# Mixed inputs of values and gate: products on ScalarE, sums on POOL, and ScalarE's order within a block

## The reference, cut to what matters

```python
xx = shift(x) - x                       # the token before minus this one
xk = x + xx * time_maa_k; xv = x + xx * time_maa_v
xr = x + xx * time_maa_r; xg = x + xx * time_maa_g
r, k, v = heads(xr @ Wr.T), heads(xk @ Wk.T), heads(xv @ Wv.T)
g = gelu(xg @ Wg.T)
# in chunks of 64 tokens, for each of 16 heads:
y  = (r @ k) * Wmat @ v + r @ state * wb
state = ws * state + (k * wk) @ v
out = (groupnorm(y) * ln_w + ln_b) * g @ Wo.T
```

## Time and profile before

| what | us |
|---|---|
| median of 3 runs (lowest, highest) | 846.95 (845.86, 848.41) |
| the profiled execution | 846.3 |
| its span, first to last instruction | 844.6 |
| busy TensorE, weight loads | 814.7, 674.5 |
| busy VectorE, ScalarE, POOL | 505.7, 464.4, 468.3 |

### The profile page before, as it was taken

One profiled execution on the slowest core, in us unless ns is written; L12 is line 12 of the kernel. 1 busy time (PEld: TensorE's weight loads), 2 busy tenths in 40 slices (PEclk: granted clock), 3 DMA queues, 4 the chain that ended last, 5 costly groups with the idle time before them and its releaser, 6 DMA issues. The chain is left out here.

```text
span 844.6 us, 17509 instructions
## 1 busy us (share of the span) xinstructions
PE 814.7 (96%) x6291; PEld 674.5 (80%) x6291; DVE 505.7 (60%) x1286; ACT 464.4 (55%) x860; POOL 468.3 (55%) x529
## 2 busy tenths in 40 slices
PE   5999999999999989899999999999999999999997
PEld 4777787777777667678998788898788899788886
DVE  6789988899998886343543543544443545353441
ACT  4478877778787667264543543644552544453331
POOL 6445577777777857475444356453436452535215
PEclk9999999999999999999999999999999999999999
DMA  5852032213111121546333334342415442413114
GB/s 163 334 209 70 28 108 68 76 52 96 40 40 48 58 91 72 178 157 135 101 70 40 110 95 70 95 113 27 124 60 79 121 106 26 95 35 44 20 14 50
DMA packets 50746, 74.30 MB, mean 88 GB/s; under 512 B 5072, under 2 KB 42448, under 8 KB 50640
## 3 DMA queue, kind: packets, MB, share of 16 engines
q1 hardware_dynamic: 35760, 53.72, 19.2%
q0 software_dynamic: 14592, 19.18, 13.6%
q10 hardware_dynamic: 288, 0.01, 0.0%
HBM read 38.67 MB, written 34.22 MB: 86 GB/s over the span
## 5 line engine op out<-in xcount | busy, mean ns | idle before, releaser
L1648 POOL DMA_INDIRECT out<-ysb,index x80 | 124.7, 1558 | 145.6 <-DVE ysb L1887 111.1
L2001 PE MATMUL p<-xh,whi 128*128 128x512 f32 (+2 forms) x504 | 185.4, 368 | 1.4 <-POOL wlo L1637 0.5
L1863 DVE TENSOR_TENSOR hid<-gated,p 128x512 f32<-128x512 f32 (+1 forms) x126 | 81.0, 643 | 176.2 <-ACT gated L1710 176.2
L2003 PE MATMUL p<-xh,wlo 128*128 128x512 f32 (+2 forms) x504 | 185.3, 368 | 0.0
L2002 PE MATMUL p<-xl,whi 128*128 128x512 f32 (+2 forms) x504 | 184.6, 366 | 0.0
L2027 PE MATMUL py<-w,hh 128*128 128x512 f32 x448 | 162.5, 403 | 4.2 <-DVE hl L1132 3.7
L1710 ACT ACTIVATE gated<-p 128x512 f32<-128x512 f32 (+1 forms) x126 | 70.8, 562 | 157.4 <-PE p L2003 152.8
L1637 POOL TENSOR_TENSOR wlo<-wraw,whi 128x448 fp32r<-128x448 f32 x56 | 70.8, 1267 | 89.8 <-ACT whi L1696 84.4
L2001 PEld LDWEIGHTS p<-xh,whi 128*128 128x128 f32 x504 | 94.7, 188 | 19.2 <-issue 3.5
L2026 PE MATMUL py<-w,hl 128*128 128x256 f32 x384 | 108.5, 283 | 0.0
L2002 PEld LDWEIGHTS p<-xl,whi 128*128 128x128 f32 x504 | 94.8, 188 | 15.2
(11 more groups left out here) (215 smaller groups left out, 1430.7 us busy)
## 6 DMA issues: line engine op xcount, KB each, us to landing
wraw<-in_w SPq DMA_DIRECT2D x24, 896.0 KB
disp<-wraw SPq DMA_DIRECT2D x16, 662.5 KB, 8.2
xtok<-disp SPq DMA_DIRECT2D x16, 530.0 KB, 4.8
x_ring<-in_x SPq DMA_DIRECT2D x16, 256.0 KB, 3.3
out<-x SPq DMA_DIRECT2D x16, 256.0 KB
xtok<-disp SPq DMA_DIRECT2D x8, 265.0 KB
out<-ysb,index POOLq DMA_INDIRECT x80
disp<-row,slot_i POOLq DMA_INDIRECT x64
```

Of the source, the lines that this page charges most:

```text
L1648: nc.gpsimd.indirect_dma_start(out, bass.IndirectOffsetOnAxis(ap=index[e.const % 2][:, t:t + 1], axis=0), ysb[j % NY][:], None, compute_op ...
L1863: nc.vector.tensor_tensor(hid[k][:, 0:w], gated[k][:, 0:w], p3[k][:, 0:w], ALU.mult).then_inc(hid_ready, 1)
L2001: nc.tensor.matmul(dst[:, 0:w], hi[m][:, wcut], xh[xcut], start=(kt == 0), stop=False)
L2003: ins = nc.tensor.matmul(dst[:, 0:w], lo[m][:, wcut], xh[xcut], start=False, stop=(kt == KT - 1))
```

## The change

For each block, the mixed inputs 2 and 3 are now made in two steps. ScalarE computes the products of both (`mixed_part`: two ACTIVATE Copy instructions with a scale for each, four in all), and POOL adds xT to each (`mixed_add`: one addition of 128 x 512 for each). VectorE's two fused instructions for values leave its loop, and POOL's two products for the gate leave POOL's. `shifted`, which overwrites diff, now waits for both additions.

Three steps of ScalarE move in its loop: `weight_high` from behind `square_y` to ahead of `turned1`; `normed2` from behind `scaled` to behind `column`; `normed1` from behind `gate` to the end. The four products stand where `normed1` stood. On POOL the scatter of tile 0 moves ahead of `gated`.

```diff
+        def mixed_add(b, k):
+            if 0 <= b < STEPS:
+                pool.wait_ge(part_ready[k], b + 1)
+                nc.gpsimd.tensor_tensor(mixed[k][:], mixed[k][:], xT[b % 2][:, :, 1:], ALU.add).then_inc(mixed_ready[k], 1)
...
             norm2(c - 2)
-            mixed_g(c + 1)
-            gated(c - 1)
             if c < TAIL - 1:
                 scatter(c - 4, range(0, 1))
+            mixed_add(c + 1, 2)
+            gated(c - 1)
+            mixed_add(c + 1, 3)
             decayed_r(c + 1)
...
+        def mixed_part(b, k):
+            if 0 <= b < STEPS:
+                act.wait_ge(diff_ready, b + 1)
+                wait(act, proj_done[k], b)
+                if b == 0:
+                    act.wait_ge(maa_in, 16)
+                for c in range(KT):
+                    ins = nc.scalar.activation(mixed[k][:, c, :], diff[:, c, :], ACT.Copy, scale=maa_sb[:, k, c:c + 1])
+                ins.then_inc(part_ready[k], 1)
...
+            weight_high(c - 4)
             turned1(c + 1)
             group_rstd(c - 1)
             logit_exp(c - 2)
             gate(c)
-            normed1(c + 2)
+            mixed_part(c + 1, 2)
+            mixed_part(c + 1, 3)
             scaled(c - 1)
-            normed2(c - 2)
             receptance(c + 1)
...
             square_y(c)
-            weight_high(c - 4)
             keep_y(c)
             column(c + 1)
+            normed2(c - 2)
             keep_logits(c + 1)
+            normed1(c + 2)
...
-                wait(dve, mixed_ready[3], b)
+                for k in (2, 3):
+                    wait(dve, mixed_ready[k], b)
...
-            mixing(c + 1, 2)
```

More of the change, by code:

```diff
@@ L408, in phase_a @@
     diff_ready = sem("diff_ready")
+    part_ready = {k: sem(f"part_ready{k}") for k in (2, 3)}
     mixed_ready = [sem(f"mixed_ready{k}") for k in range(4)]
@@ L577, in decayed_r @@
                     rdecay[:].unsqueeze(2).to_broadcast([P, KT, TPS, Q]), ALU.mult).then_inc(rdec_ready, 1)
-        def mixed_g(b):
+        def mixed_add(b, k):
             if 0 <= b < STEPS:
[L581 to L588, removed]
+                pool.wait_ge(part_ready[k], b + 1)
+                nc.gpsimd.tensor_tensor(mixed[k][:], mixed[k][:], xT[b % 2][:, :, 1:], ALU.add).then_inc(mixed_ready[k], 1)
         def weight_low(i):
```

## The result

The changed kernel takes 852.62 us (median of 7 runs, 850.73 to 854.85), the kernel before beside it 845.86 (7 runs). The ratio is 1.0073, with a 95% interval of 1.0057 to 1.0089. The forecast of 843.5 was wrong, and so was its range: the time lies 5.2 us above the end of it, and 3.2 above the one rival that was slower than before. The profiled execution took 850.73, with a span of 848.5 where the kernel before has 844.6.

A forecast was written before the change was run, and what follows sets the result against it. TensorE's own list was taken to bound the attention at 18.03 us a block, with the expert stage untouched. Terms 1.9 + 1.2 + 0.5 - 0.1 = 3.5 us off 846.3 gave 842.8, median 843.5; range 841.3 to 847.4.

The forecast's parts named there:

- What bounds the kernel: Attention blocks: TensorE's own list sets 18.03 us a block; nine blocks can give back about 4.1 us.
- state_a and the masks: Loop blocks: state_a runs ahead of POOL's addition, 0.4 us instead of 1.24; TensorE's wait for masks goes: 1.9 us off.
- The residual's lag: Ahead of group sums: r_dec starts earlier and stops holding back the residual addition: 1.2 us off, bounds 0 and 1.2.
- ScalarE and z: Loop blocks: ScalarE can hold four more products; zg is ready 0.3 us before TensorE wants it.
- I count all of this at 0: Loop blocks: the other moved steps of ScalarE and POOL cost nothing, except 0.1 us lost for zg.
- The first: Rival, group sums: the residual's lag is not POOL's and stays; 1.2 us of the sum goes: 844.7; chance 0.17.
- The second: Rival, loop: state_a meets the new addition, r_dec still holds the residual; 0.4 us is left: 846.5; chance 0.20.
- The third: Rival: z behind four products makes project_o wait 0.45 us in each of 13 blocks: 849.4; chance 0.08.
- The fourth: Rival: waits for k_dec shrink as well, and the last block gives 1.1 us: 842.0; chance 0.10.
- Start, end and expert stage: Block from 279.81 gives 0.5 us, bounds -0.5 and 1.1; start-up, written-out end and expert stage keep their times.

The follow-up runs named there:

- The kernel that has all of it: Changed kernel with all four scatters ahead of POOL's first addition, and k_dec ahead of logit_max and stats2 on VectorE: 838.21 us, 0.9915 of before.
- 841.27: Changed kernel with POOL's weight piece moved ahead of the scatter of tile 1: 841.27 us, 0.9944 of before.
- 839.49: Changed kernel with all four scatters of a block moved ahead of POOL's first addition: 839.49 us, 0.9931 of before.
- a run that left POOL alone: Kernel before the change, with k_dec moved ahead of logit_max and stats2 on VectorE: 845.07 us, 0.9984 of before.
- the run with one input: Changed kernel with L1118 taking the counts in PSUM instead of slotf in SBUF, leaving the capacity rule out of the slots: 848.36 us, 1.0025 of before.

## Why the prediction was wrong, step by step

**What bounds the kernel.** Right: a block of 18.03, about 4.1 us to be had in nine blocks, and no more. The kernel that has all of it shows it.

**state_a and the masks.** Right in mechanism and size. The pair takes 0.41 and starts at T+5.6, ahead of the first addition by 1.0 us; the masks no longer wait. The prediction had a POOL addition hold a VectorE instruction with two inputs in SBUF, and this held wherever the runs put the two together. The pair of state_b (L1029) now meets zg (L617): the pair ends at 199.10 and zg at 199.05, and it takes 1.42 instead of 0.40, which the prediction didn't mention; it falls ahead of the residual's wait of 1.79 and costs nothing.

**The residual's lag.** The size is right, -1.3 against -1.2, and the reason isn't shown. The prediction had r_dec hold the residual, because the residual began 0.37 to 0.44 us after it. With k_dec earlier in the kernel before, r_dec begins as near or nearer, and there is no lag. With the piece ahead of the DMAs the residual begins 0.56 to 0.60 us into the weight piece in eight blocks, and is on time and takes 0.42. The lag went in every run of another kernel but for 0.1 us where the values are back on VectorE, whose pair ends late there. So this term came out by luck, as far as the runs tell: what made the residual late in the kernel before stays open.

**ScalarE and z.** Right. zg is ready at T+9.67, and TensorE takes it at T+10.36: the cover is 0.7 where the prediction had 0.3, because four products take 1.69 and the next starts after 1.60, not 1.98:

```profile
194.97 1.69 ACT L685 ACTIVATE mixed<-diff,maa_sb 128x256 f32<-128x256 f32 x4
196.57 1.08 ACT L821 ACTIVATE z<-yn,lnb_sb,lnw_sb 128x256 f32<-128x256 f32 x2
```

**The step that failed** is "I count all of this at 0", of what the change moves on POOL. The prediction had looked for who waits for each moved step, and found nobody early enough. It had not looked for what each POOL instruction now runs beside. It had both facts for it: that POOL holds small VectorE instructions until its end, and that the weight piece does so to L1075. It applied them to state_a and the residual, and never walked down VectorE's list for instructions that weren't late yet. What the runs showed in place of the 0: the product L1118, or one of the three ahead of it, is held for 1.6 to 1.8 us in each of eight blocks, k_dec is late behind it, and scores wait 11.2 us more.

That walk would have been close, too. By the prediction's own times r_dec starts at T+11.3, so that the second DMA of tile 1 starts at about T+14.1, and the product, 1.33 us behind the residual at T+12.4, at T+13.7: free, by 0.3 us. In the run r_dec starts at T+10.68. The 0.6 are from two durations taken from rows of before that were too long: 0.49 a product instead of 0.40, four times, and 1.28 an addition instead of 1.08. Both errors were on the side that makes the forecast safe for z, and unsafe for the slots. A walk would have put the product within 0.3 us of the last DMA. It still would have had to guess what follows there, for the product begins 0.6 us before the weight piece does, and no row of the kernel before shows an instruction held by a POOL instruction that hadn't begun: in the middle blocks the same product ran inside a DMA in 0.17. What the walk could have given is a rival with a chance of its own, priced at 1.4 us in eight blocks.

**The rivals.** The first, that the lag isn't POOL's, is borne out as far as r_dec goes, and not in its result: the lag didn't stay. The second, the collision moved and not removed, is what happened, but it was tied to state_a and r_dec, where it could only give back what was gained, hence its 846.5. The third, slower, had a mechanism that the run with ScalarE's old order shows at 3.9 us, but the changed kernel doesn't reach it. The fourth said that the waits for k_dec shrink; they grew from 0.85 to 12.0 us.

**Start, end and expert stage.** The last loop block and what follows gave 2.9, against a forecast of 0.5 with a bound of 1.1, and the start 0.6. The 2.9 is a term that the prediction had too small. From the start of the last loop block to the expert stage it is 63.7 us before, and 60.6 to 61.8 in the changed kernel and in nine of the ten made from it; it is 64.1 only with the first scatter back. That points to the scatter's place, but the same run has a held product in the last loop block too, so it isn't shown. With the hold gone it is most of what puts 841.27 and 839.49 below the forecast of 843.5. The 0.6 and the 0.7 are no more than differences between executions: over all fourteen kernels the nine blocks begin at 112.4 to 114.6, and the expert stage, which is the same in all, takes 499.2 to 501.0.

## What to carry to other kernels

When a step moves on POOL, walk down VectorE's whole list beside POOL's new row, not only the instructions that wait now: a small instruction that takes 0.2 us can be held as long as the POOL instruction that it meets, and what counts is what stands between it and the next engine that waits. If such a walk comes out free by less than the error of its durations (0.6 us here), the collision is a rival with a price of its own. Two remedies worked without removing any work: let an indirect DMA, not a long read, stand where VectorE has its small instructions (-11 us), and put what TensorE waits for right behind them (-7.6). And a constant distance between two instructions isn't a cause: the residual's, steady over nine blocks, vanished in a run that left POOL alone.

## What the runs showed of the hardware

- A VectorE instruction of 16 numbers, started 0.4 to 0.7 us into a POOL indirect DMA of 0.98 us, isn't done before the long POOL instruction behind that DMA: up to 1.9 us, and an end 0.04 behind the weight piece's or r_dec's. With a gap of 0.30 behind the DMA (started 0.6 in), or small instructions (128x2) behind it (started 0.4 in), it takes 0.17. By the profile's times the weight piece hadn't begun when the product did.
- Not every such instruction is held. In the kernel with all scatters early and k_dec earlier, state_a's pair (two inputs in SBUF) begins 0.55 us into a DMA with an addition 0.01 behind it, in two blocks, and takes 0.25 each. That addition still waited for ScalarE's first products, which ended at 154.93, after the pair; the weight piece waited for nothing. This fits a hold that begins when POOL's next instruction is ready, but the two cases differ in more than that, and it wasn't tested. DVE and POOL:

```profile
153.78 1.49 POOL L605 DMA_INDIRECT disp<-row,slot_i  x1 [0.30 <-issue]
...
154.33 0.41 DVE L1015 SCALAR_TENSOR_TENSOR state<-state,sdecay,kvm 128x32 f32<-128x32 f32 x2
...
155.28 1.11 POOL L583 TENSOR_TENSOR mixed<-mixed,xT 128x512 f32<-128x512 f32 x1
```

- Some single-input instructions from SBUF to SBUF are held as well: the cast of 128x4 1.32 us, the `tensor_scalar` of 128x8 1.59. The MAX8 of 128x8 is not: it begins 0.6 us into the same DMA in the run with one input, and takes 0.17.
- A DMA alone holds the cast, to its own end: begun 0.51 us into one with the 0.30 gap behind it, in the run with r_dec early, it takes 0.46. A `tensor_scalar` does the same in the kernel before (0.43, from 146.44), and the product right behind it ends with it; hence the 0.31 and 0.36 of the product in two blocks.
- A Copy of 128x256 with a scale per partition follows the one before it on ScalarE after 0.40 us, against 0.49 for xn and z, which have a bias too. POOL's addition of 128x512 takes 1.08 in the changed kernel, and took 1.28 in the one before; why wasn't tried.
